# Second wide attention of a four-layer block: projections as three products of f16 halves

## The reference

```python
def _L2_xattn_ref(x, context, ln_gamma, ln_beta, w_q, w_kv, w_out, b_out, gate):
    xn = _layernorm(x, ln_gamma, ln_beta)
    q = (xn @ w_q).reshape(B, SQ, NUM_HEADS, DIM_HEAD)
    kv = context @ w_kv
    k, v = jnp.split(kv, 2, axis=-1)
    ...
    scores = jnp.einsum('bqhd,bkhd->bhqk', q * SCALE, k)
    attn = jax.nn.softmax(scores, axis=-1)
    out = jnp.einsum('bhqk,bkhd->bqhd', attn, v).reshape(B, SQ, INNER)
    out = out @ w_out + b_out
    return out * jnp.tanh(gate[0])
```

## Time and profile before

| | us |
|---|---|
| median of three runs | 602.95 |
| the profiled execution | 600.79 |
| its span (first to last instruction) | 598.7 |
| TensorE busy in the span | 527.3 (88%) |
| VectorE busy | 449.2 (75%) |
| ScalarE busy | 344.9 (58%) |
| POOL busy | 217.3 (36%) |

### The profile page before, as it was taken

One profiled execution on the slowest core, in us unless ns is written; L12 is line 12 of the kernel. 1 busy time (PEld: TensorE's weight loads), 2 busy tenths in 40 slices (PEclk: granted clock), 3 DMA queues, 4 the chain that ended last, 5 costly groups with the idle time before them and its releaser, 6 DMA issues.

```text
span 598.7 us, 13027 instructions
## 1 busy us (share of the span) xinstructions
PE 527.3 (88%) x4784; PEld 304.3 (51%) x4792; DVE 449.2 (75%) x1251; ACT 344.9 (58%) x672; POOL 217.3 (36%) x214
## 2 busy tenths in 40 slices
PE   8889999997878799988996789688999999898896
PEld 3345555555843123333333467435666566754584
DVE  5989999998368679927876799867777776496653
ACT  3578888887144156644751768448888878222112
POOL 2047777778120000000002547206777778200100
PEclk9989999999999779999998999989999999999969
DMA  8770000004010000000000211000000000000000
GB/s 220 144 210 2 3 1 2 2 2 142 2 36 0 2 1 2 1 2 2 1 1 18 88 54 54 2 1 1 1 2 2 2 2 2 2 1 1 1 0 19
DMA packets 24082, 15.40 MB, mean 26 GB/s; under 512 B 8083, under 2 KB 22230, under 8 KB 23894
## 3 DMA queue, kind: packets, MB, share of 16 engines
q1 hardware_dynamic: 24022, 14.60, 9.2%
HBM read 14.33 MB, written 0.26 MB: 24 GB/s over the span
## 4 chain that ended last, share of the span: by engine, by line
PE 40%; issue 29%; DVE 18%; ACT 9%; POOL 3%; DMA 0%; DVEq 0%; POOLq 0%; ACTq 0%
PE psM L433 4%; PE pspair L483 3%; DVE Zt L1524 3%; ACT PP L1181 3%; PE pspair L632 3%; PE pspair L885 2%; PE psS L457 2%; PE psO L657 2%; PE psO L501 2%; DVE Oall L1782 2%; PE psS L405 2%; PE pspair L373 2%; DVE Oall L1572 1%; ACT PP L1165 1%; PE pspair L405 1%
## 5 line engine op out<-in xcount | busy, mean ns | idle before, releaser
L2193 POOL TENSOR_TENSOR ln_rs<-ln_ve,minus_half 128x4 f32<-128x4 f32 x10 | 10.2, 1023 | 225.0 <-DVE ln_ve L1411 221.8
L483 PE MATMUL pspair<-ident,PP 128*128 128x128 f32 x528 | 84.0, 282 | 7.8 <-ACT PP L1181 4.3
L483 PEld LDWEIGHTS pspair<-ident,PP 128*128 128x128 f32 x528 | 57.4, 140 | 50.5 <-issue 41.9
L501 PE MATMUL psO<-V,PP 128*128 128x64 f16 x1536 | 65.0, 193 | 11.7 <-DVE Oall L1572 9.8
L501 PEld LDWEIGHTS psO<-V,PP 128*128 128x128 f16 x1536 | 60.3, 98 | 17.1 <-DVE PP L1537 13.4
L1537 DVE TENSOR_TENSOR PP<-pspair,PP 128x512 f16<-128x512 f32 x68 | 46.8, 688 | 27.5 <-ACT PP L1165 27.4
L1239 ACT ACTIVATE PP<-pspair 128x1024 f32<-128x1024 f32 x48 | 46.6, 1023 | 30.3 <-PE pspair L643 30.2
L1181 ACT ACTIVATE PP<-scores_m,nm 128x512 f32<-128x512 f32 x68 | 49.5, 728 | 17.5 <-DVE nm L1511 13.9
L2202 POOL TENSOR_TENSOR PP<-acc,one 128x512 f16<-128x512 f32 x32 | 33.3, 1039 | 72.0 <-ACT acc L1163 71.8
L1165 ACT CAST PP<-pspair 128x512 f16<-128x512 f32 x68 | 39.6, 583 | 4.5 <-PE pspair L483 4.5
L2202 POOL TENSOR_TENSOR PP<-y_sb,one 128x512 f16<-128x512 f32 x32 | 33.3, 1039 | 19.5 <-ACT y_sb L1163 19.4
(11 more groups left out here) (497 smaller groups left out, 1224.8 us busy)
## 6 DMA issues: line engine op xcount, KB each, us to landing
W<-in_L_ffn_W SPq DMA_DIRECT2D x16, 256.0 KB, 2.9
bigw<-in_L_xattn_w_q SPq DMA_DIRECT2D x2, 512.0 KB, 5.7
bigw<-in_L_xattn_w_kv SPq DMA_DIRECT2D x1, 1024.0 KB, 5.6
V<-in_ctx SPq DMA_DIRECT2D x1, 512.0 KB, 3.9
bigw<-in_L_xattn_w_v SPq DMA_DIRECT2D x1, 512.0 KB, 5.9
mask_b<-in_mask_BxS_ff SPq DMA_DIRECT2D x1, 512.0 KB, 8.1
bigw<-in_L_xattn_w_k SPq DMA_DIRECT2D x1, 512.0 KB, 6.4
bigw<-in_L_xattn_w_o SPq DMA_DIRECT2D x1, 512.0 KB, 4.0
```

The lines of the kernel that those rows point to most:

```text
L483: mm = pe.transpose(bank[f"T{j % 2}"][:, k * P:(k + 1) * P], Pb[j % 4][:, k * P:(k + 1) * P], ident[:])
L501: mm = pe.matmul(bank["O"][:, (j % UPH) * a.dv:(j % UPH + 1) * a.dv], (PTH, PTL)[ppart][j % 4][:, k * P:(k + 1) * P], values_of(a)[vpart][ ...
```

## The change

Keys and queries of L2X are made out of f16 halves, three products each in place of one f32 product; L0X keeps its f32 products. POOL forms the halves of the context (into `ctxTm`, as `C16`), of the key weights (into `kT1`, as `W16[1]`) and of the query weights (into `W1[0]` and `W1[1]`, as `W16[0]`), each with one operation of 128x1024 for the high half and one for the low half: the context's after the first `m16` of L1X, the key weights' after the last repeated keys of L1F, the query weights' after the last expert's splits. The turned x is no longer copied as f32: ScalarE writes its high half, VectorE its low half, the latter between the low halves of V13 and V14 in VectorE's program. The values are made as before.

```diff
--- before.py
+++ after.py
@@ -308,6 +308,9 @@
         KW = maskf.bitcast(F16)
         zero_m = [Zt[:].bitcast(BF16)[:, k * SK:(k + 1) * SK] for k in range(2)]
         P32 = [t[:].rearrange("p t d -> p (t d)") for t in (acc, y_sb)]
+        C16 = ctxTm[:].bitcast(F16)
+        WK16 = kT1[:].bitcast(F16)
+        W16 = [[W1[k][:].bitcast(F16) for k in range(2)], [WK16[:, 0:INNER], WK16[:, INNER:2 * INNER]]]
         Kst = [KW, Amat[:, 0:8, :].rearrange("p a c -> p (a c)").bitcast(F16)]
         K32 = tmp[:].rearrange("p t d -> p (t d)")
         minus16 = G[:, 0, 0, :].bitcast(F16)
@@ -380,16 +383,28 @@
                 mm = pe.transpose(ps[:, t * P:(t + 1) * P], src[:, t, :], ident[:])
             mm.then_inc(full["M"], 1)
 
-        def pe_first_keys(pe, a, src, load):
-
-            pe.wait_ge(sem(load), 2 * 16)
+        def projection(pe, a, ps, what, k, moving):
+
+            side, cols_ = (0 if what == "Q" else 1), slice(k * P, (k + 1) * P)
+            if a.mask:
+                return pe.matmul(ps[:], bigw[:, side, cols_], moving, start=True, stop=(what != "rest"))
+            for m, (wpart, xpart) in enumerate(PARTS):
+                part = X16[:, xpart, :] if what == "Q" else \
+                    C16[:, xpart * CTX + (what == "K1") * SK:xpart * CTX + (what == "K1") * SK + SK]
+                mm = pe.matmul(ps[:], W16[side][wpart][:, cols_], part, start=(m == 0), stop=(m == 2))
+            return mm
+
+        def pe_first_keys(pe, a, src):
+
             for b in range(B):
-                pe_one(pe, f"{a.name}.K{b}", f"T{b}", bigw[:, 1, 0:P], src[:, b * SK:(b + 1) * SK])
+                ps = take(pe, f"{a.name}.K{b}", f"T{b}")
+                projection(pe, a, ps, f"K{b}", 0, src[:, b * SK:(b + 1) * SK]).then_inc(full[f"T{b}"], 1)
 
         def pe_first_query(pe, a, xT):
 
             emptied(pe, f"{a.name}.xt")
-            pe_one(pe, f"{a.name}.Q", "M", bigw[:, 0, 0:P], xT[:])
+            ps = take(pe, f"{a.name}.Q", "M")
+            projection(pe, a, ps, "Q", 0, xT[:]).then_inc(full["M"], 1)
 
         def pe_wide_values(pe, L, parts, banks="S0 S1 S2 S3"):
 
@@ -429,9 +444,8 @@
 
                 m = {"K0": 0, "rest": 1, "Q": a.per - 2, "K1": a.per - 1}[what]
                 reuse(f"{n}.proj", a.per * (PPI * i + k - 1) + m)
-                side, moving = {"Q": (0, xT[:]), "K1": (1, KT[:, SK:2 * SK])}.get(what, (1, KT[:, 0:SK]))
-                mm = pe.matmul(bank["M"][:], bigw[:, side, (PPI * i + k) * P:(PPI * i + k + 1) * P], moving, start=True,
-                               stop=(what != "rest"))
+                moving = {"Q": xT[:], "K1": KT[:, SK:2 * SK]}.get(what, KT[:, 0:SK])
+                mm = projection(pe, a, bank["M"], what, PPI * i + k, moving)
                 if what == "rest":
                     mm = pe.matmul(bank["M"][:], minus16, Kst[k][:, 0:SK], start=False, stop=True)
                 mm.then_inc(full["M"], 1)
@@ -907,8 +921,11 @@
 
         def pe_l2x(pe):
             pe_wide_values(pe, "L2", range(6, 2 * NC))
-            pe_first_keys(pe, L2X, ctxT, "ld.L2")
+            pe.wait_ge(sem("L2.c16"), 1)
+            pe.wait_ge(sem("L2.wk16"), 1)
+            pe_first_keys(pe, L2X, ctxT)
             pe_ln(pe, "L2x", XN[1])
+            pe.wait_ge(sem("L2.wq16"), 1)
             pe_first_query(pe, L2X, XT[1])
             pe_attention(pe, L2X, ctxT, XT[1], [f"L2.V{v}" for v in range(2 * NC)])
             pe.wait_ge(sem("ld.L2wo"), 16)
@@ -1106,7 +1123,8 @@
                 emptied(pe, f"ctxT{g}")
             pe_wide_values(pe, "L0", range(0, NC))
             pe.wait_ge(sem("L0x.ctx"), 1)
-            pe_first_keys(pe, L0X, ctxTm, "ld.L0")
+            pe.wait_ge(sem("ld.L0"), 2 * 16)
+            pe_first_keys(pe, L0X, ctxTm)
             pe_first_query(pe, L0X, XT[0])
             pe_wide_values(pe, "L0", range(NC, 2 * NC))
             pe_attention(pe, L0X, ctxTm, XT[0], [f"L0.V{v}" for v in range(2 * NC)])
@@ -1345,7 +1363,7 @@
             act_moe(act)
             act_wide_values(act, "L2", range(6, 2 * NC))
             act_first_keys(act, L2X)
-            act_copy(act, "L2x.xt", XT[1][:])
+            act_high(act, "L2x.xt", X16[:, 0, :])
             act_first_query(act, L2X)
             act_attention(act, L2X)
             act_out(act, L2X, NPAIR)
@@ -1876,7 +1894,10 @@
             def l2x():
                 ln_gain("L2b", X, "L2_xattn_ln_gamma", lambda t: rowp["L2_xattn_ln_beta"], XN[1], "L2x.xn",
                         lows("L2", range(7, 8)), twice_normed=True)
-                for step in lows("L2", range(8, 16)):
+                for step in lows("L2", range(8, 14)):
+                    step()
+                low("L2x.xt", X16[:, 1, :], X16[:, 0, :])
+                for step in lows("L2", range(14, 16)):
                     step()
                 first_keys(L2X)
                 first_query(L2X)
@@ -2271,7 +2292,18 @@
             rstd("L0f")
             selectors()
             rstd("L1x")
+            pool.wait_ge(sem("L1x.m16"), 1)
+            filled(pool, "L0x.proj", L0X.per * (NPAIR - 1) - 1)
+            pool.tensor_tensor(C16[:, 0:CTX], ctxT[:], one[:].broadcast_to([P, CTX]), ALU.mult).then_inc(sem("L2.chigh"), 1)
+            pool.wait_ge(sem("L2.chigh"), 1)
+            pool.tensor_tensor(C16[:, CTX:2 * CTX], ctxT[:], C16[:, 0:CTX], ALU.subtract).then_inc(sem("L2.c16"), 1)
             rstd("L1f")
+            pool.wait_ge(sem("ld.L2"), 2 * 16)
+            filled(pool, f"L1f.RK{NG - 1}.0")
+            pool.tensor_tensor(W16[1][0], bigw[:, 1, :], one[:].broadcast_to([P, INNER]), ALU.mult)\
+                .then_inc(sem("L2.wkhigh"), 1)
+            pool.wait_ge(sem("L2.wkhigh"), 1)
+            pool.tensor_tensor(W16[1][1], bigw[:, 1, :], W16[1][0], ALU.subtract).then_inc(sem("L2.wk16"), 1)
             rstd("L1fn")
 
             def split_W2(i, k2, first):
@@ -2297,6 +2329,11 @@
             with pool.Fori(1, E // 2) as i:
                 for k2 in range(2):
                     split_W2(i, k2, False)
+            pool.wait_ge(sem("moe.w1"), E)
+            pool.tensor_tensor(W16[0][0], bigw[:, 0, :], one[:].broadcast_to([P, INNER]), ALU.mult)\
+                .then_inc(sem("L2.wqhigh"), 1)
+            pool.wait_ge(sem("L2.wqhigh"), 1)
+            pool.tensor_tensor(W16[0][1], bigw[:, 0, :], W16[0][0], ALU.subtract).then_inc(sem("L2.wq16"), 1)
             rstd("L1gn")
             rstd("L2b")
             pool_attention(L2X)
```

## The result

The changed kernel takes 610.35 us, median of 20 runs (603.47 to 614.43); 20 runs of the kernel before, taken beside it, have a median of 603.0 (598.89 to 605.58). The ratio is 1.0109, 95% interval 1.0082 to 1.0136: slower by 1.1%, some 7 us.

A forecast was written before the change was run, and what follows sets the result against it. The prediction took TensorE as nearly the bound in L2X's loop, a software pipeline turning once per head pair. Its terms, -4.7 + 0.7 + 0 + 1.4 + 1.7, summed to -0.9 us, giving 602.0 us, range 598.3 to 606.5.

The forecast's parts named there:

- Part 1: L2X loop: products in three f16 halves save 0.68 us per pair of heads, 4.7 us in all.
- The rival that the pipeline does not give it back: L2X loop: shorter products only let TensorE wait longer, so half of 4.7 us is gained; 604.4 us, chance 0.18.
- Part 2: Start of L2X: VectorE's new order makes the query's low half, and so all scores, later; +0.7 us.
- two gaps of 1.4 and 2.3: Start of L2X: TensorE idles 1.4 us before the query product and some 2.3 before the next, from 0.82 and 1.49.
- Part 3, context: L1X: POOL's context halves end before VectorE's next short operations of the kind it can hold; no hit, 0.
- Part 3, key weights: L1F: POOL's low half holds VectorE's tensor_tensor, and the delay goes through whole; +1.4 us.
- Part 3, query weights: Mixture's last expert: POOL's high half takes the gap after two low halves, delaying VectorE's last two and TensorE's outputs; +1.7 us.
- That the clock may fall: L2X's start, secondly the mixture: TensorE's clock halves after longer idle gaps; price 4 us, 606.0 us, chance 0.18.

The follow-up runs named there:

- experiment 11: Experiment 8 plus unread spare TensorE products, five ahead of L2X's first query product and six behind it; 595.01 us, ratio 0.9891 to the kernel before.
- experiment 2: Changed kernel with POOL's query-weight halves after the experts' last low halves and key-weight halves after L1F's last spread; 598.19 us, ratio 0.993 to the kernel before.
- experiment 8: Experiment 2 with the low half of x written after all the values' low halves; 601.12 us, ratio 0.9865 to the kernel before.
- experiment 3: Changed kernel with 18 unread spare products on TensorE ahead of the last expert's last outputs; 606.08 us, ratio 1.007 to the kernel before.
- experiment 7: Changed kernel with POOL's key- and query-weight halves cut into pieces of 128x256, at the same places; 602.84 us, ratio 1.0011 to the kernel before.
- experiment 10: Experiment 8 plus unread spare products, ten ahead of V12, five ahead of the first query product, six behind it; 601.6 us, ratio 0.9952 to the kernel before.
- experiment 1: Changed kernel with only POOL's query-weight halves delayed until after VectorE's last low half of the experts' hidden layers; 603.13 us, ratio 1.0013 to the kernel before.
- experiment 12: Experiment 11 run again for its interval; 595.14 us, ratio 0.9898 to the kernel before.
- experiment 9: Experiment 8 run again for its interval; 601.37 us, ratio 0.9988 to the kernel before.

## Why the prediction was wrong

**Part 1, right.** From the first query in the loop to the seventh, six turns, the trace has 407.97 to 490.94 before and 421.36 to 500.26 after: 13.83 and 13.15 a turn, 0.68 less, which is the forecast term to its digits. From the first row maximum of L2X to its end, experiment 11 with the clock up takes 120.06 and before took 124.44: 4.4, where 4.7 was forecast. The rival that the pipeline does not give it back is ruled out.

**Part 2, right in its steps, one step short.** The query's low half starts 3.70 after the start of x's high half, where the earlier trace rows have 2.56 for the f32 copy and the working gave 3.62 (397.98 to 401.6); two gaps of 1.4 and 2.3 were named, and 1.62 and 2.09 measured. The clock fell behind them (412 to 420). From L2X's root to the first row maximum it took 18.00 us where it had been 15.63, so +2.4 where +0.7 was forecast. Experiments 2, 8 and 11 take it apart: 17.64 with both pairs of operations late, 16.75 with x's low half behind the values' besides, 15.48 with the eleven spares and so with the clock up. The order is worth 0.9 and the clock 1.3, the latter shown by the spares alone; the 0.4 between 18.00 and 17.64 is not taken further apart.

**Part 3, context: right.** L1X's stage is unchanged.

**Part 3, key weights: +3.1 for +1.4.** The wait is nearly as sized (1.28 for 1.35), but by luck. It was the tensor_scalar that was held, not the tensor_tensor behind it, and POOL's two operations ended 4.1 us after their start and not 4.4; the two errors offset each other. The Trainium skill (GPSIMD Engine Reference, Key points) counts a VectorE operation in a 2-port mode as one that contends, beside those with two SBUF inputs. The trace agrees as far as it goes, with 1.70 us in place of 0.17, though it does not show the mode, and my own reading of the earlier trace rows, that only two-input operations are held, was too narrow. The other 1.8 is the clock behind the wait. All six traces with POOL's operations at this place have a stretch at half clock between 304 and 312, and none of the other eight has.

**Part 3, query weights: +6.0 for +1.7. This is the step that failed, twice over.** First, "VectorE works off two low halves until 376.61" was taken as one closed block: POOL was given only the gap behind it, 1.1 us after the end of its last split (375.46), and only its high half was counted as a hit. In truth POOL stood in line at once, came in at the first handover between two operations of VectorE, and again at the second, so both its long operations hit: 3.4 us of stall. Second, stalls of TensorE were priced at their own length. Behind this one the clock was at half for 2.4 us' worth more (experiment 3 gives exactly this back). That the clock may fall was among the rivals, with the gap of 2.7 us in the mixture named as its second place; I gave it 0.18 and 4 us for the whole. It was the right mechanism, and it came in all three stages: 1.8 in L1F, 2.4 in the mixture, some 1.7 at the start of L2X (2.4 less the forecast's 0.7). It was wrong to let it stand as a case of its own beside the forecast: each of the three terms that made TensorE wait longer here brought it along.

**The sum as it came out:** -4.4 + 0.7 + 1.3 + 3.4 for products and waits is +1.0; +5.9 for the clock behind the waits makes +6.9. The medians differ by 7.35. Without the clock, then, the forecast of -0.9 would have been off by 2, by the second hold in the mixture; the clock made a small loss into a plain one.

## What to carry to other kernels

A long POOL operation on SBUF can hold VectorE's next SBUF operation for its whole length, and VectorE's own work does not keep it out. Put it where VectorE reads PSUM or idles, or cut it in pieces (experiment 7: 7.5 us of 610 for a changed loop). Price a wait of TensorE at its length plus the clock that may fall behind it. Where a gap must stay, a handful of spare products in it can help, if they are placed while the clock is still up and fit in the gap (experiments 3 and 11; the ten of experiment 10 came too late).

## What the runs showed of the hardware

- POOL's operation of 128x1024 took 1.89 and 2.13 us, less than twice that of 128x512 (1.039 and 1.16), if not held.
- The hold goes both ways and in turn: POOL's own operations took 2.34 and 2.45 in the mixture, and the additional 0.45 and 0.3 lie under VectorE's low halves. VectorE's records leave no gap there (the second starts at 380.65, the first ends at 380.73), and POOL still came in between.
- Held were tensor_tensors with two SBUF inputs, and a tensor_scalar (1.70 for 0.17) and a cast (0.61 for 0.18, experiment 7) with one. Not held were a reciprocal in SBUF (0.25) and what reads PSUM (row maxima 0.68).
- Gaps of TensorE of 1.2 (L1F), 4.45 (mixture), and 1.62 with 2.09 (L2X) were each followed by a stretch at half clock, and so was one of 0.90 in L1F (experiment 7); gaps of 1.02 and of 2.07 in the last expert (experiments 1 and 7) were not. So the gap's length alone does not decide.
- The clock also differs between executions of equal code. From the last root to the end, where no kernel here differs from another, it took 37.2 us before, 38.9 in the changed kernel, 35.5 in experiments 1, 11 and 12, and 41.4 in experiment 9, as the clock had it. L1F took 55.49 in experiment 9 with no operation of POOL's near, the clock being at half from 281 to 292. The busy table by stretch of the changed kernel near its end:

```profile
596.00:608.00 12.00, 9.20 (x36) 5.40 (x34) 2.58 (x10) 0.49 (x2) 0.54 (x1) 0.53 0.03 10
```

  The sum of a single trace of this kernel can thus be off by several us. A stage says more, but only where several traces agree. What makes the clock fall there, and at 150 to 180 and 281 to 292 in some of the traces, stays open: it was not tried.
